# Wider moving operands for the small matmuls of an attention and expert kernel, and five changes of order on three engines

## The reference

```
z  = layernorm(x)
q  = z @ Wq + bq ;  k = z @ Wk + bk                  # 16 heads of 16 features
q_w = softmax over the rows of (q @ Wqa + bqa) / 4    # one weight per row and head
pooled_q = sum over rows of q_w * q
mixed  = k * pooled_q
k_w = softmax over the rows of (mixed @ Wka + bka) / 4
pooled_k = sum over rows of k_w * mixed
x = x + (pooled_k * q) @ Wt + bt + q

f  = rmsnorm(layernorm(x)) * norm_weight
shared = relu(f @ sw1 + sb1) @ sw2 + sb2              # 256 -> 1024 -> 256
p  = sigmoid(f @ router_w.T) ; the two best of 8 experts per row, weights normalised
x = x + shared + sum over the two experts of weight * (relu(f @ ew1 + eb1) @ ew2 + eb2)
```

## Time and profile before

| what | value |
| --- | --- |
| median of three runs | 762.47 us (761.93 to 764.41) |
| the profiled execution | 762.13 us, of it 760.3 us span from the first to the last instruction |
| mean granted TensorE clock | 0.986 of full speed |
| PE busy | 721.7 us, 95% |
| DVE busy | 558.7 us, 73% |
| ACT busy | 438.3 us, 58% |

### The profile page before, as it was taken

The page is one execution under the profiler, slowest core; times in us unless marked ns, Lnnn a source line. Parts: engine busy times, 40 slices in busy tenths (PEclk is TensorE's granted clock), DMA queues, the critical chain, the costliest instruction groups (busy, mean ns, idle before and its releaser), DMA issues. The chain is left out here.

```text
span 760.3 us, 11580 instructions
## 1 busy us (share of the span) xinstructions
PE 721.7 (95%) x4238; PEld 602.8 (79%) x4238; DVE 558.7 (73%) x1114; ACT 438.3 (58%) x739; POOL 180.8 (24%) x156
## 2 busy tenths in 40 slices
PE   2789898899999999999999999999999999999997
PEld 2546666687888888989888889889888989888786
DVE  5624676689856777688687878678777878677994
ACT  3631335653465658494765776595846695757432
POOL 1100011000003124334424425333424343220000
PEclk9889999999999999999999999999999999999999
DMA  9400112003001536445465656455555755353970
GB/s 320 165 1 1 57 56 83 28 1 118 1 1 42 191 105 215 158 160 172 158 216 188 197 164 235 156 198 160 167 161 186 248 170 180 108 185 116 302 225 28
DMA packets 45945, 106.93 MB, mean 141 GB/s; under 512 B 9309, under 2 KB 33888, under 8 KB 38336
## 3 DMA queue, kind: packets, MB, share of 16 engines
q1 hardware_dynamic: 39072, 88.49, 35.1%
q0 software_dynamic: 6816, 17.71, 7.0%
HBM read 89.39 MB, written 17.69 MB: 141 GB/s over the span
## 5 line engine op out<-in xcount | busy, mean ns | idle before, releaser
L901 ACT ACTIVATE hid<-psU,b 128x512 f32<-128x512 f32 (+2 forms) x280 | 154.6, 580 | 189.5 <-issue 141.2
L648 PE MATMUL psD<-w,hhi 128*128 128x512 f32 x824 | 214.2, 400 | 4.1 <-ACT hhi L904 1.9
L1241 DVE TENSOR_TENSOR hlo<-hid,hhi 128x512 fp32r<-128x512 f32 x206 | 139.4, 690 | 74.0 <-ACT hhi L904 72.1
L648 PEld LDWEIGHTS psD<-w,hhi 128*128 128x128 f32 x824 | 146.9, 188 | 37.2 <-ACT hhi L904 4.1
L630 PE MATMUL psU<-xhl,w 128*128 128x512 f32 (+2 forms) x560 | 146.2, 342 | 0.0
L624 PE MATMUL psU<-xhl,w 128*128 128x512 f32 (+2 forms) x560 | 146.0, 342 | 0.0
L626 PE MATMUL psU<-xhl,w 128*128 128x512 f32 (+2 forms) x560 | 145.8, 342 | 0.0
L403 POOL DMA_INDIRECT xin<-token_in,src x71 | 79.0, 1112 | 251.9 <-PE psT L600 131.4
L1276 DVE TENSOR_TENSOR w<-raw,w 128x1024 fp32r<-128x1024 f32 x112 | 132.7, 1216 | 1.8 <-ACT w L794 1.8
L411 POOL DMA_INDIRECT token_out<-fold,dst x71 | 87.7, 1235 | 141.4 <-DVE fold L1270 131.5
L654 PEld LDWEIGHTS psD<-w,hlo 128*128 128x128 f32 x824 | 110.1, 188 | 9.3 <-DVE hlo L1241 0.3
(11 more groups left out here) (195 smaller groups left out, 515.3 us busy)
## 6 DMA issues: line engine op xcount, KB each, us to landing
raw<-in_wpack SPq DMA_DIRECT2D x58, 1024.0 KB, 5.4
xT<-token_out SPq DMA_DIRECT2D x32, 256.0 KB, 5.3
x_sb<-in_x SPq DMA_DIRECT2D x8, 512.0 KB, 9.1
token_in<-z_sb SPq DMA_DIRECT2D x8, 512.0 KB, 3.2
out<-x_sb SPq DMA_DIRECT2D x16, 256.0 KB, 5.5
b<-in_b2pack SPq DMA_DIRECT2D x29, 128.0 KB, 5.4
att<-in_attn SPq DMA_DIRECT2D x1, 1379.0 KB, 10.1
xin<-token_in,src POOLq DMA_INDIRECT x71, 2.9
```

What stands on the lines that cost most here:

```text
L648: mm(acc, hhi[:, part], wpair[slot][:, :, c * D:(c + 1) * D], start=(c == 0), stop=False)
L901: last = nc.scalar.activation(hid[:, n % 4, i * rows:(i + 1) * rows], acc, ACT.Relu, bias=b1[:, u % 2, m:m + 1])
L1241: V.tensor_tensor(hlo[:, part], hid[:, n % 4, :], hhi[:, part].bitcast(F32), ALU.subtract).then_inc(hlo_ready, 1)
```

## The change

Six things are edited.

1. Every matmul of 1, 16 or 32 columns in the attention moves 128 columns instead, the same ones repeated by a broadcast read: `fold_query`, `fold_key`, `spread_max`, the sum at the end of `pool_rows`, `project_pooled`. The results that are read stand where they did or in strided places of the psD bank; the columns of psD are laid out anew for that.
2. In `project` the bias matmul and its wait for `crow_ready` stand behind the eight weight matmuls, and the first of those starts the accumulation.
3. `folded_query` on VectorE moves behind `stats_of(4)`, `offsets(1)` and `normalise_even(8, 16)`.
4. On TensorE the transposes of z and the projections 10 to 13 alternate, and `router(0)` comes behind projection 13 instead of ahead of projection 12.
5. `ranks()` comes behind the third quarter of group 0's `down` instead of the second.
6. In the first quarter of `down` of the last three S groups the last `hhi` matmul comes behind six of the `hlo` matmuls.

```diff
-        C_FOLD = C_HEAD + KD * NH
-        C_MAX, C_SUM, C_SB = C_FOLD + KD * 32, C_FOLD + KD * 32 + 1, C_FOLD + KD * 32 + 2
+        C_FOLD, C_SB, C_SUM, C_MAX = 0, 2 * P, 2 * P, 3 * P
+
+        def wide(ap, n):
+            return ap.rearrange("p (o n) -> p o n", o=1).to_broadcast([ap.shape[0], P // n, n])
...
-                        mm(psD[:, b, C_FOLD + 32 * k:C_FOLD + 32 * k + 32], wkT[:, n, k * P:(k + 1) * P], gk[:, n, b, :],
+                        mm(psD[:, b, C_FOLD + k * P:C_FOLD + (k + 1) * P], wkT[:, n, k * P:(k + 1) * P], wide(gk[:, n, b, :], 32),
                            start=(n == 0), stop=(n == KD - 1))
                 for g in range(4):
                     for n in range(KD):
-                        last = mm(psD[32 * g:32 * g + 32, b, C_SB:C_SB + 1], gk[:, n, b, :],
-                                  att[:, A_BK + n:A_BK + n + 1], start=(n == 0), stop=(n == KD - 1))
+                        last = mm(psD[32 * g:32 * g + 32, b, C_SB:C_SB + P], gk[:, n, b, :],
+                                  att[:, A_BK + n:A_BK + n + 1].to_broadcast([P, P]), start=(n == 0), stop=(n == KD - 1))
...
-                    last = mm(psD[32 * g:32 * g + 32, b, C_MAX:C_MAX + 1], mrow[0:1, b, :], ones[0:1, 0:1],
+                    last = mm(psD[32 * g:32 * g + 32, b, C_MAX:C_MAX + P], mrow[0:1, b, :], ones[0:1, 0:P],
                               start=True, stop=True)
...
-                mm(psD[:, b, C_SUM:C_SUM + 1], sel, small[:, b, 5:6], start=True, stop=True).then_inc(pooled_ps[b], 1)
+                mm(psD[:, b, C_SUM:C_SUM + P], sel, small[:, b, 5:6].to_broadcast([P, P]), start=True, stop=True).then_inc(pooled_ps[b], 1)
...
-                        last = mm(psD[:, b, C_HEAD + NH * n:C_HEAD + NH * (n + 1)], wmat[:, k, n * P:(n + 1) * P],
-                                  pool_sb[:, b, k, :], start=(k == 0), stop=(k == KD - 1))
+                        last = mm(psD[:, b, C_HEAD + n * P:C_HEAD + (n + 1) * P], wmat[:, k, n * P:(n + 1) * P],
+                                  wide(pool_sb[:, b, k, :], NH), start=(k == 0), stop=(k == KD - 1))
...
                 if q % (NT // 4) == 0:
                     pe.wait_ge(m_ready[b], 1)
-                    pe.wait_ge(crow_ready[b], 1)
                 pair = psU[:, proj_bank[q], :].rearrange("p (t n) -> p t n", t=2)
-                mm(pair, one2[:, :], cpair[:, b:b + 1, :].to_broadcast([2, 2, D]), start=True, stop=False)
                 for tt in range(2):
                     t = 2 * q + tt
                     for k in range(KD):
-                        last = mm(pair[:, tt, :], xT[:, t // 4, k, t % 4 * P:(t % 4 + 1) * P], mt[:, b, k, :],
-                                  start=False, stop=(tt == 1 and k == KD - 1))
+                        mm(pair[:, tt, :], xT[:, t // 4, k, t % 4 * P:(t % 4 + 1) * P], mt[:, b, k, :],
+                           start=(tt == 0 and k == 0), stop=False)
+                if q % (NT // 4) == 0:
+                    pe.wait_ge(crow_ready[b], 1)
+                last = mm(pair, one2[:, :], cpair[:, b:b + 1, :].to_broadcast([2, 2, D]), start=False, stop=True)
...
+                    late = kinds[g] == "S" and g > SA and q == 0
...
-                    if g == 0 and q == 1:
+                    for c in range(MH - 1 if late else MH):
+                        high(c)
+                    if late:
+                        for c in range(MH - 2):
+                            rest(c)
+                        high(MH - 1)
+                    for c in range(MH - 2 if late else 0, MH):
+                        last = rest(c)
+                    if g == 0 and q == 2:
                         ranks()
...
             first_moments(1)
-            folded_query()
             stats_of(4)
             offsets(1)
             normalise_even(8, 16)
+            folded_query()
             first_moments(2)
```

More of the change, by code:

```diff
@@ L450, in fold_query @@
                     for n in range(KD):
-                        mm(psD[:, 0, C_FOLD + 32 * k:C_FOLD + 32 * k + 32], wqT[:, n, k * P:(k + 1) * P], wqa[:, n, :],
+                        mm(psD[:, 0, C_FOLD + k * P:C_FOLD + (k + 1) * P], wqT[:, n, k * P:(k + 1) * P], wide(wqa[:, n, :], 32),
                            start=(n == 0), stop=(n == KD - 1))
@@ L454, in fold_query @@
                     for n in range(KD):
-                        last = mm(psD[32 * g:32 * g + 32, 0, C_SB:C_SB + 1], wqa[:, n, :],
-                                  att[:, A_BQ + n:A_BQ + n + 1], start=(n == 0), stop=(n == KD - 1))
+                        last = mm(psD[32 * g:32 * g + 32, 0, C_SB:C_SB + P], wqa[:, n, :],
+                                  att[:, A_BQ + n:A_BQ + n + 1].to_broadcast([P, P]), start=(n == 0), stop=(n == KD - 1))
                 last.then_inc(fold_ps, 1)
@@ L640, in down, with high @@
                     acc = psD[:, n % 2, :].rearrange("p (s n) -> p s n", s=2)
-                    for c in range(MH):
+                    late = kinds[g] == "S" and g > SA and q == 0
+                    def high(c):
                         if q == 0 and c * rows % 512 == 0:
@@ L648, in down, with rest @@
                         mm(acc, hhi[:, part], wpair[slot][:, :, c * D:(c + 1) * D], start=(c == 0), stop=False)
-                    for c in range(MH):
+                    def rest(c):
                         if q == 0 and c * rows % 512 == 0:
@@ L652, in down @@
                         part = slice(c * rows + q * P, c * rows + (q + 1) * P)
-                        col = slice(c * D, (c + 1) * D)
-                        last = mm(acc[:, 1, :], hlo[:, part], whi[slot][:, col], start=False, stop=(c == MH - 1))
+                        return mm(acc[:, 1, :], hlo[:, part], whi[slot][:, c * D:(c + 1) * D], start=False, stop=(c == MH - 1))
+                    for c in range(MH - 1 if late else MH):
[6 more added lines that the diff above has]
+                        last = rest(c)
                     last.then_inc(down_done, 1)
-                    if g == 0 and q == 1:
+                    if g == 0 and q == 2:
                         ranks()
@@ L723, in _ @@
             turn_z(4)
+            project(10)
             turn_z(5)
-            project(10)
+            project(11)
             turn_z(6)
+            project(12)
             turn_z(7)
-            project(11)
+            project(13)
             router(0)
-            project(12)
-            project(13)
             turn_z(8)
@@ L1030, in folded_query @@
                 dve.wait_ge(fold_ps, 1)
-                V.tensor_copy(aq[:].rearrange("p k h -> p (k h)"), psD[:, 0, C_FOLD:C_FOLD + KD * 32])
+                V.tensor_copy(aq[:], psD[:, 0, C_FOLD:C_FOLD + KD * P].rearrange("p (k h) -> p k h", k=KD)[:, :, 0:32])
                 for b in range(B):
@@ L1084, in own_head @@
                 dve.wait_ge(headed_ps[b], r + 1)
-                link(V.tensor_tensor(dtmp[:, b], psD[:, b, C_HEAD:C_HEAD + KD * NH].rearrange("p (n h) -> p n h", n=KD),
+                link(V.tensor_tensor(dtmp[:, b], psD[:, b, C_HEAD:C_HEAD + KD * P].rearrange("p (n h) -> p n h", n=KD)[:, :, 0:NH],
                                      hm, ALU.mult))
@@ L1097, in folded_key @@
                 dve.wait_ge(key_ps[b], 1)
-                V.tensor_copy(bk_[:, b].rearrange("p k h -> p (k h)"), psD[:, b, C_FOLD:C_FOLD + KD * 32])
+                V.tensor_copy(bk_[:, b], psD[:, b, C_FOLD:C_FOLD + KD * P].rearrange("p (k h) -> p k h", k=KD)[:, :, 0:32])
                 V.tensor_tensor(small[:, b, 0:1], psD[:, b, C_SB:C_SB + 1], att[:, A_BKA:A_BKA + 1],
```

## The result

| kernel | median us | lowest to highest | runs | ratio to before, 95% interval |
| --- | --- | --- | --- | --- |
| before | 762.51 | 758.20 to 764.45 | 6 | |
| after | 754.12 | 752.83 to 754.99 | 6 | 0.9895 [0.987, 0.9919] |

The change takes 8.4 us. The forecast was 5.3 (757.2 us, range 754.6 to 761.6): the direction was right, and the time lies 0.5 us under the range. The profiled execution of after took 754.99 us, the slowest of its six, and that of before 762.13, a little under its median, so profile against profile the gain is 7.14. The other 1.2 us are in no trace here.

What follows compares the result with a forecast made beforehand. TensorE, busy 721.7 of 760.3 us, was taken as the bound. The terms summed to -5.25 from the profiled 762.13, giving 756.9, and 0.34 for the median made 757.2 us; range 754.6 to 761.6.

Steps and rivals of the forecast that it cites:

- the cost of the wide matmuls: 128-column small matmuls on TensorE, queuing within a column group: fold_key +2.8 us, spread_max +0.95, longer tails of full-weight ones +0.8.
- the second stretch: Low-clock stretch at 29 to 33 us: full speed gains 1.0 us, GpSimd's late power takes 0.6 back, net -0.4.
- rival C: Wide matmuls overlap fully, so the 2.8 becomes 0.4 and the 0.95 becomes 0.1: 754.0 us, chance 0.08.
- VectorE's start: Without VectorE's wait for the folded query, TensorE's transposes start at 18.2 instead of 19.35 us: -1.15 us.
- The clock: Of five low-clock stretches in the first 126 us, four reach full speed: -1.5, -0.4, -1.7, -3.25 us; the fifth stays.
- Rival A: The clock falls in the second to fourth stretch as before: slower, 763.5 us, chance 0.1.
- Rival B: One clock fall remains, a new one comes, or the fifth stretch lengthens: 759 to 760.5 us, chance 0.2.
- Bias last: Projections 0 and 8 no longer wait for the bias row ahead of their weight matmuls: -0.75 us each.
- The router: Router two projections later; logits_out(0) ahead of the odd z rows on ScalarE lets 3.5 of 4.95 us through: +1.45 us.
- Ranks: With one more quarter of group 0's down ahead, TensorE's wait for VectorE's one-hot rows goes: -1.3 us.
- Last groups: Six hlo matmuls run before the last hhi matmul, so the last group's quarter ends earlier: -0.45 us.
- Rival D: The gain is lost because VectorE is late in 155 to 200 us or at the end: 761 to 762.5 us, chance 0.12.

Runs made afterwards that it cites:

- all_but_wide: after with the small matmuls back at 1, 16 and 32 columns instead of 128; median 756.94 us, ratio 0.9966.
- logits_later: after with logits_out(0) on ScalarE moved behind z_outs(8, 12) instead of ahead of z_rows_odd(2); median 748.95 us, ratio 0.9842.
- all_but_late: after with the last hhi matmul back in its old place in the last groups; median 754.01 us, ratio 0.989.
- wide_only: before with only the small matmuls widened to 128 columns; median 760.02 us, ratio 0.997.

## Why the prediction was off, step by step

**The step that failed is the cost of the wide matmuls**: "Only the last of one group lies beside the first of the next: 4 x (3 x 0.12 + 0.03) and a tail of 0.1 is 1.65, so +1.4, twice". The instructions of a group do take 0.11 each, but those of the other groups run beside them, four in a row or not: start to next start is 0.60 where it was 0.26 at the narrow width (66.13 to 66.39 in all_but_wide), the same as in before (39.49 to 39.75), so +0.34, twice, not +2.8 but +0.7. `spread_max` went by the same assumption: 0.35 us (41.74 to 42.09) instead of 0.17 (45.35 to 45.52 in before), +0.18 each, not +0.5. The full-weight ones were about right: `project_pooled` and the sum +0.1, that part of `fold_key` +0.1 to +0.2, seven in all, some 0.8. The term of 4.55 us measures about 1.9. That is 2.6 us. Profile against profile the whole miss is 1.9 (7.14 instead of 5.25), so the other terms lost some 0.7 against it, above all the 0.4 of the second stretch and the 0.5 in the last group. This is the mechanism of rival C, which had 0.08. That the median lies within 0.2 us of C's price, 754.0, is luck: profile against profile C says 8.45 us, and 7.14 were measured.

**VectorE's start**: forecast 18.2 for the transposes, measured 17.53; `fold_query` too took 0.60 instead of 1.65. But to the score it is 3.81 us, not 3.0: ScalarE is at the odd rows until 18.72 and its four copies then set the pace. The score came 2.52 us earlier, and -1.15 - 1.5 had said 2.65. Right in sum, with what was won at the start lost at ScalarE: that two misses cancel is luck.

**The clock**: the third and fourth stretch stayed up. The fourth gave 3.15 us of 3.25, and the third's score takes 1.92. The second did not in the profiled run; its 0.4 were not won. Rival A fell. Rival B came true in part: one of the falls stayed, and against the sum that cost only the 0.4. The reading that the falls inside 39 to 44 and 53 to 61 us came with TensorE busy was taken from the stretches in which the clock was down already. Ahead of the third TensorE was busy, 3.35 of 4 us; ahead of the fourth, which begins at 53.5 us, it had waited 0.60 and 0.44 us for ScalarE.

**Bias last**: forecast -1.5, measured 0.8 and 0.6. Up to projection 8 the trace has 7.2 us instead of 4.95; the 2.6 of the wide term less the 0.4 of the second stretch is that difference.

**The router**: forecast +1.45. 7.2 us came in and 5.7 went on, 1.5, through the very order on ScalarE that was named. What the prediction did not ask was whether that order had to stand: without the wait behind it the fifth fall is gone as well, and both together are 4.6 us (logits_later).

**Ranks**: forecast -1.3. The lead grows by 7.28 - 5.7 = 1.6 us over that stretch, and undone alone the edit is worth 1.5 at its place, so it was right or a little small; the 1.0 of the times has an uncertainty larger than the difference. **Last groups**: forecast -0.45, in the trace -0.33, in the times nothing. In after's profiled run a transfer was late there as well (`xT<-token_out`, 0.28 us of wait for VectorE at 732.96), and in all_but_late's none was. The rest of the 0.5 us given back there is not assigned. **Rival D** fell: from 160 to 700 us the lead stays within 0.2 us.

**The range** ended at 754.6, 0.5 us too high. The low bounds of the wide terms had been worked out, but they stood as rival C (754.0) with 0.08, and the range left a part of C out.

The sum of the leave-one-out values is 3.4 + 5.0 - 1.8 + 2.3 + 1.0 - 0.1 = 9.8 us against 8.4 measured. The difference is within their uncertainty, and they need not add up: after a fall is gone by one edit, another edit has less left to gain.

What stays open: which run falls where, and by what about the columns the clock stays up. before varies by 7 us over 29 runs, logits_later by 1.2 over five, and a profile shows one execution.

## What to carry to other kernels

Price small matmuls in different column groups by the longest group, not by the sum; that is shown for four in a row to each group, and for 16 in a row in the first. When TensorE's clock falls, look at what it did ahead of the fall and not during it, when everything takes longer and looks busy. Where there was no wait ahead and the instructions there move few columns, repeating columns is worth a try if the output has room: it brought 3.4 and 5.6 us here. When a producer is moved later on one engine, read the list of the engine that consumes it: what stands behind the consumer there pays, and moving it a few lines may be worth more than the change itself.

## What was not expected of the hardware

- Four column groups work through 16 instructions of 128 columns in 0.60 us when each group has its four in a row, 0.58 us in turn, and 12 more in one group take 0.11 us each; the other groups then begin only when that one has four left.
- The clock fell at 39.8 us in before behind 4 us with 3.35 busy, in which 32 of 42 instructions moved 1 to 32 columns, and stayed up in logits_later behind 4 us with 2.56 busy and 128 columns or more in each. Over six runs the mean clock of the kernel with the later logits was 0.984 to 0.995 with narrow columns, over five 0.997 to 1.0 with wide ones.
- In wide_only the clock stayed at 0.50 for 10 us with TensorE busy throughout.
- The times of the kernel whose profiled run has no fall are also closer together: 1.2 us from lowest to highest over five runs, against 7 us over 29 for before (a range grows with the number of runs, and after itself has 2.2 over six).
